# Four buffers for the attention's residual, with other banks, another steady order and another order of the first slots

## What is computed

```python
x = x + tanh(g_xattn[0]) * performer(layernorm(x), ctx, ctx)
x = x + tanh(g_ffn[0]) * ffn(layernorm(x))
# performer: 16 heads of 16, 64 random features, causal
proj_q, proj_k = (q * scale) @ random_features, (k * scale) @ random_features
h_k = -0.5 * sum(k * k);  k_stab = max(h_k)          # over all batches
q_prime = nc * (exp(proj_q) + 1e-4)
k_prime = nc * (exp(h_k + proj_k - k_stab) + 1e-4)
out = causal(q_prime @ k_prime.T) @ v / causal(q_prime @ k_prime.T).sum()
# ffn: attention of each token over its own 16 heads, then a soft mixture of 8 experts
x = x + (softmax(q @ k.T / 4) @ v) @ Wo + bo
gate = softmax(rmsnorm(x) @ Wg + bg)
return x + sum_e gate[e] * (rmsnorm(x) @ We[e])
```

## Time and profile before

| | us |
|---|---|
| median of 3 runs | 1058.45 (1058.41 to 1059.62) |
| the profiled execution | 1063.04 |
| its span | 1061.3 |
| TensorE busy in the span | 984.1 (93%) |
| VectorE, ScalarE, GpSimd busy | 885.9 (83%), 763.1 (72%), 793.3 (75%) |
| scores of batch 0, 4 and 7 begin | 45.74, 142.18, 239.16 |
| scores of batch 31 begin | 973.56 |

### The profile page before, as it was taken

How to read it: one execution, slowest core, us unless ns; L and a number is a source line. 1 busy time by engine, 2 the same in 40 slices (tenths; PEclk the granted TensorE clock), 3 DMA queues, 4 the chain that set the end, 5 groups by cost and what they waited for, 6 DMA issues and landing times.

```text
span 1061.3 us, 35315 instructions
## 1 busy us (share of the span) xinstructions
PE 984.1 (93%) x14918; PEld 824.8 (78%) x14918; DVE 885.9 (83%) x1860; ACT 763.1 (72%) x1628; POOL 793.3 (75%) x1275
## 2 busy tenths in 40 slices
PE   0467899999999999999999999999999999999998
PEld 0346678888878888888888888888888888888787
DVE  6777888888988888889888888888888889887887
ACT  5669876678777777877767777776777877776541
POOL 4478887777878778778787877778778777887551
PEclk9989999999999999999999999999999999999999
DMA  9600001100111100101110000011100101100000
GB/s 294 188 22 22 29 15 32 32 12 22 32 32 32 32 21 23 32 22 32 32 32 32 13 31 24 30 32 32 32 29 15 32 22 32 32 22 12 12 12 31
DMA packets 39439, 38.89 MB, mean 37 GB/s; under 512 B 3953, under 2 KB 39025, under 8 KB 39281
## 3 DMA queue, kind: packets, MB, share of 16 engines
q1 hardware_dynamic: 38896, 36.59, 11.0%
q0 software_dynamic: 384, 0.04, 0.1%
HBM read 28.23 MB, written 8.39 MB: 35 GB/s over the span
## 4 chain that ended last, share of the span: by engine, by line
PE 65%; POOL 14%; DVE 9%; ACT 4%; DMA 4%; issue 3%; SPq 1%; POOLq 0%; ACTq 0%
PE ps L2454 12%; PE ps L2456 11%; PE ps L2455 11%; PE ps L2499 7%; PE ps L2487 6%; PE ps L2469 4%; PE ps L2448 4%; PE ps L2533 3%; DMA c_in<-in_ctx 3%; PE ps L2509 2%; PE ps L2524 2%; DVE z L1528 2%; PE ps L2492 2%; DVE hk L1866 1%; POOL x L466 1%
## 5 line engine op out<-in xcount | busy, mean ns | idle before, releaser
L1528 DVE SCALAR_TENSOR_TENSOR z<-ps,gate,z 128x256 f32<-128x256 f32 x512 | 239.6, 473 | 28.6 <-POOL gate L550 16.2
L2454 PE MATMUL ps<-we_hi,h_hi 128*128 128x512 f32 (+2 forms) x640 | 237.9, 372 | 0.3 <-DVE qkv L1645 0.3
L2456 PE MATMUL ps<-we_hi,h_lo 128*128 128x512 f32 (+2 forms) x640 | 224.4, 351 | 0.0
L2455 PE MATMUL ps<-we_lo,h_hi 128*128 128x512 f32 (+2 forms) x640 | 224.1, 350 | 0.0
L2487 PE MATMUL ps<-qf,kf 64*64 64x192 f32 (+1 forms) x2048 | 152.2, 365 | 16.9 <-POOL kf L581 4.0
L2454 PEld LDWEIGHTS ps<-we_hi,h_hi 128*128 128x128 f32 x640 | 120.4, 188 | 26.5 <-issue 10.5
L2456 PEld LDWEIGHTS ps<-we_hi,h_lo 128*128 128x128 f32 x640 | 120.3, 188 | 17.3
L2455 PEld LDWEIGHTS ps<-we_lo,h_hi 128*128 128x128 f32 x640 | 120.8, 189 | 11.7
L2492 PEld LDWEIGHTS ps<-qf,kf 64*64 64x64 f32 x2048 | 106.3, 136 | 6.4
L2499 PE MATMUL ps<-att,v 128*32 128x256 f32 (+1 forms) x2048 | 103.4, 332 | 2.1 <-POOL att L521 1.2
L2492 PE MATMUL ps<-qf,kf 64*64 64x128 f32 (+1 forms) x2048 | 100.9, 247 | 0.0
(11 more groups left out here) (231 smaller groups left out, 3042.6 us busy)
## 6 DMA issues: line engine op xcount, KB each, us to landing
x_in<-in_x SPq DMA_DIRECT2D x32, 256.0 KB, 2.8
c_in<-in_ctx SPq DMA_DIRECT2D x64, 128.0 KB, 3.0
out<-z SPq DMA_DIRECT2D x32, 256.0 KB, 2.2
c_chunk<-in_ctx SPq DMA_DIRECT2D x14, 512.0 KB, 5.6
stage<-in_L_ffn_We SPq DMA_DIRECT2D x2, 1024.0 KB, 11.6
c_chunk<-in_ctx SPq DMA_DIRECT2D x2, 256.0 KB, 3.8
stage_o<-in_L_ffn_Wo SPq DMA_DIRECT2D x1, 256.0 KB, 3.5
stage_q<-in_L_ffn_Wq SPq DMA_DIRECT2D x1, 256.0 KB, 12.7
```

The costliest lines, as they stand in the source:

```text
L1528: return dve.scalar_tensor_tensor(out=z[b % 2][:, t, :], in0=ps[:, bank, offset:offset + D], scalar=gate[:, t, ex:ex + 1], in1=z[b % 2][:, ...
L2454: pe.matmul(out, a_hi(c), b_hi(c), start=(c == 0), stop=False)
L2455: pe.matmul(out, a_hi(c), b_lo(c), start=False, stop=False)
L2456: last = pe.matmul(out, a_lo(c), b_hi(c), start=False, stop=(c == C - 1))
```

## The change

It has four parts; kinds, sizes and number of the computing instructions stay the same.

- `x1` has four buffers where it had two. Its step no longer waits for `z0` of two batches before, and waits for `o_x` in every batch. In POOL's slot it moves from behind `z0` to behind `o_n`.
- `BANK` gives other banks to `av0`, `fk0`, `fk3`, `fq0`, `fq1`, `fq2`, `fq3`, `kv1`, `mm01`, `mm0g`, `mm1g`, `o`, `qq`, `s`, `x010`, `x011`, `x110`, `x111`, `y01`, `y10`, `y11`. The semaphores are grouped anew and the conditional waits follow the new orders.
- The slot of each engine has another order. SP's issues the context first and the store last. POOL's puts `k_lo` and `m11`, besides `g_r`, `m10` and `r2`, ahead of `v_bd`, and gate, v1, pk2, m00, m01, q_r at its end, which is where the next period begins. DVE's has `q_bn` ahead of `g_bn`, and `c_t` behind `a01`. ACT's has `k_bd` ahead of `x000`. PE's changes a few neighbours (`mm1g` for `mm0g` first, `kv1` ahead of `kv0`, `mm12` ahead of `mm11`).
- The first slots are written in another order, with more of them written out on PE, POOL and ACT; their last parts are now part of the loop's order. On PE, `mm03` stands right behind `mm02` for batch 31, and behind only `h2_t.31` for batch 30, where `mm11` and `mm12`, or others, stood between them.

```diff
-BANK = dict(av0=0, av1=3, dn=5, first=0, fk0=0, fk1=6, fk2=4, fk3=5, fq0=4, fq1=2, fq2=7, fq3=3, h2=0, ht=1, kv0=7,
-            kv1=6, mm00=4, mm01=0, mm02=7, mm03=7, mm0g=0, mm10=5, mm11=6, mm12=3, mm13=6, mm1g=1, nd0=2, nd1=3, o=4,
-            otr=4, pv0=1, pv1=2, qq=1, s=5, stab=0, x000=1, x001=7, x010=5, x011=4, x100=4, x101=2, x110=7, x111=3,
-            y00=0, y01=2, y10=1, y11=6)
+BANK = dict(av0=5, av1=3, dn=5, first=0, fk0=5, fk1=6, fk2=4, fk3=0, fq0=2, fq1=3, fq2=4, fq3=7, h2=0, ht=1, kv0=7,
+            kv1=3, mm00=4, mm01=2, mm02=7, mm03=7, mm0g=1, mm10=5, mm11=6, mm12=3, mm13=6, mm1g=0, nd0=2, nd1=3, o=2,
+            otr=4, pv0=1, pv1=2, qq=6, s=0, stab=0, x000=1, x001=7, x010=2, x011=5, x100=4, x101=2, x110=6, x111=1,
+            y00=0, y01=4, y10=7, y11=3)
...
-        x1 = [sb(f"x1_{p}", [P, T, D]) for p in range(2)]
+        x1 = [sb(f"x1_{p}", [P, T, D]) for p in range(4)]
...
-                store_(n - 4)
-                load_x_(n + 2)
                 load_c_(n + 3)
+                load_x_(n + 2)
+                store_(n - 4)
...
-                if b in (0, 1, 4):
-                    pool.wait_ge(*at("o_x", b))
-                if b >= 2:
-                    pool.wait_ge(*at("z0", b - 2))
-                pool.tensor_tensor(x1[b % 2][:, :, :], o_x[:, :, :], x_in[b % 2][:, :, :], ALU.add).then_inc(*up("x1", b))
+                pool.wait_ge(*at("o_x", b))
+                pool.tensor_tensor(x1[b % 4][:, :, :], o_x[:, :, :], x_in[b % 2][:, :, :], ALU.add).then_inc(*up("x1", b))
...
-                if b in (3, 4, 29, 30, 31):
-                    pool.wait_ge(*at("v_t", b))
+                pool.wait_ge(*at("v_t", b))
```

2459 lines of the change are left out of this document (1433 added, 1026 removed).

## The result

| | median, us | runs |
|---|---|---|
| before | 1060.77 (1058.09 to 1064.85) | 22 |
| after | 1065.59 (1061.74 to 1068.41) | 22 |

The ratio is 1.0042 [1.0031, 1.0052]: 0.4% slower, where 1055.0 and "faster" were forecast. The forecast started from 1058.45, the median of 3 runs of the kernel before; over these 22 it is 1060.77, and 2.3 of the 10.6 us between 1055.0 and 1065.59 are that difference. The profiled execution of the changed kernel took 1066.27 us, 1064.3 of them in the span, 0.7 above its median; the one of before was 2.3 above the median of these 22 runs.

A forecast was written before the change was run, and what follows sets the result against it. Bound: mostly TensorE's own work in the steady part, with waits at the start, in four batches and the tail. Terms −3.3 − 3.0 + 1.4 + 1.5 = −3.4 took 1058.45 to 1055.0 us; range 1047 to 1061.5.

The forecast's parts named there:

- Start, −3.3: Up to batch 0's scores: VectorE fills and a statistic moved into idle time save 4.2, POOL's added steps cost 0.9.
- Slots 0 to 3, −3.0: Batches 0 to 3: 2.3 us from ACT's scalings and q_lo.1 moved, 0.7 more by batch 4; bounds −5 to +1.
- that is 2.3 us on the scores of batch 1: Batch 0: two ACT weight scalings leave the exponentials' way, q_lo.1 fills POOL's idle time; batch 1's scores gain 2.3 us.
- Steady part, +1.4: 24 regular periods: −5.8 from c_in waits gone, +7.2 from pv waiting for POOL's v_bd; bounds −5.8 to +5.
- 24 × 0.3: Steady part: POOL's longer chain to v_bd starts pv 0.3 us late in each of 24 periods, +7.2.
- what is then late is nothing on this engine: Steady part, VectorE: context load issued first ends 14 c_in waits; TensorE returns to 30.36 us periods, up to −5.8.
- x1 and banks, 0: Steady part: four x1 buffers worth nothing themselves; other banks cost 0, bounded at 0 to 0.1 us a period.
- Tail, +1.5: After the steady part: TensorE waits of 3.9 to 5 us (mm03, mm1g, pv) against 3.0 before; bounds 0 to +3.
- A: Rival, steady part: POOL's chain keeps up and v_bd never holds pv; −10.6, 1047.9 us; chance 0.20.
- C: Rival, steady part: v_bd costs over 0.5 us each period; at 0.6, +3.8, 1062.3 us, slower; chance 0.16.
- B: Rival: gains of start and slots 0 to 3 given back before steady part; +0.9, 1059.4; 0.26 with forecast's upper edge.
- D: Rival: steady part unchanged at 30.60 us a period; 1053.7 us, inside the forecast; chance 0.38 together with the forecast.

The follow-up runs named there:

- b_fill: Kernel before with the new kernel's start on VectorE (fills and first statistic ahead of c_t.0, sel_h ahead of first sum) and load_x.0 first: 1057.95 us, ratio 0.9968.
- a_fill: Kernel after with its VectorE start put back (fills, first statistic and sel_h behind the first context and first sum): 1073.09 us, ratio 1.009 to the kernel before.
- a_wehi: Kernel after with ACT's scalings we_hi3 and we_hi1 put back between batch 0's score tiles, gamma2 ahead of the stabilizer: 1067.19 us, ratio 1.0037 to the kernel before.
- b_x1: Kernel before with x1 in four buffers instead of two, its step not waiting for z0 of two batches before: 1061.52 us, ratio 0.9988.

## Why the prediction was wrong

**Start, −3.3: right.** −3.4 in the profile. As an edit of its own (b_fill) it gave −3.9, and 0.32% of the whole; POOL's order is left alone there, so by the prediction's sum it would be the −4.2 of VectorE. The sum of fills taken out of VectorE's busy chain was a sound way to read the earlier trace rows. It does not tell what the old order costs in the new kernel (7.1, a_fill).

**Slots 0 to 3, −3.0: wrong.** +0.3. The step that failed is "that is 2.3 us on the scores of batch 1", added to a layout with old durations. The scores of batch 1 did come earlier in the profile (17.98 us behind batch 0, where it was 20.12). But the scalings were not what had held them: put back (a_wehi), they moved the scores of batch 1 by 1.0 at most. And the gain did not last: batch 2 took 28.02 us where it had taken 24.50, and TensorE's idle time over the four batches stayed at 20 to 21 us. The prediction's bounds allowed for this, a wait of one engine for another "may take it all". Two executions of the kernel after differ by 2.6 us here (96.74 and 94.15) with the clock, so a term of 3 us in this stretch can't be read from one pair of profiles' lengths.

**Steady part, +1.4: wrong by 2.8.** It came at +4.2 in this pair, and at some +7 over the eight profiles named under the result. V_bd was sized right in the loop: 0.3 forecast, 0.34 measured by the move of k_lo. What failed was (a) "24 × 0.3" as the whole price of the new order. Only 17 of the 24 periods run in POOL's loop order; seven are written out in another, and four of them, 10 to 13, took 2.8 us more than before. In three of those pv waited for v_bd as well, 0.20 to 0.39, behind waits for x and for the stored z that the sum has no term for. The section on the change says that more slots were written out, but the prediction let the loop's order stand for them. And (b) "what is then late is nothing on this engine; TensorE comes back to the regular 30.36". The load of x was put behind a load that waits, and its first reader put ahead of g_bn; when x lands late, the period is 31.4 to 32.5. Nor were the c_in waits worth 5.8: alone, in the kernel before, taking them away gave back 1.0 to 3.2. The last 16 periods came out at +1.8 where the prediction's figure for 24, +1.4, would give +0.9.

**x1 and banks, 0: right** as far as tried; x1 was (b_x1).

**Tail, +1.5: right in kind and nearly in size,** +1.9. The waits named are there, on TensorE's timeline of the new kernel:

```profile
1009.83 1.16 PE L2804 MATMUL ps<-v_bd,p_t 128*32 128x68 f32 x64 [1.13 <-DVE ht_lo L2083]
...
1029.84 1.15 PE L2804 MATMUL ps<-v_bd,p_t 128*32 128x68 f32 x64 [0.86 <-DVE z L1803]
1032.99 0.39 PE L2725 MATMUL ps<-we_hi,h_hi 128*128 128x264 f32 x1 [0.71 <-DVE h_lo L1859]
...
1046.82 0.39 PE L2725 MATMUL ps<-we_hi,h_hi 128*128 128x256 f32 x1 [0.73 <-DVE z L1803]
...
1059.48 0.39 PE L2725 MATMUL ps<-we_hi,h_hi 128*128 128x256 f32 x1 [1.17 <-DVE z L1803]
```

The last two are mm03 of 30 and of 31, put at 0.6 and 1.1; the 0.71 is mm1g.30. The five add up to 4.6, within the 3.9 to 5 of the forecast, but in part by luck: the mis-sized terms are pv, 0.4 each in the forecast and 1.13 and 0.86 here, and the 0.7 for mm1g.31, which didn't come. With h2_t put ahead of pv and mm13.29 ahead of mm1g.30 the tail is 1.3 shorter.

**Rivals.** A fell with pv's 0.34. C had the right sign by another road: it asked for more than 0.5 a period at v_bd, and v_bd stayed at 0.34; the written-out periods and the late x made up the rest. B's mechanism was right as to batches 0 to 3 and no more. D kept the steady mean at 30.60; it came at 738.61 / 24 = 30.78.

**What stays open.** The medians differ by 4.8 us and the two profiled executions by 3.2. The other profiles of the two steady orders say that this pair is a mild one (+7.2 over batches 7 to 30, not +4.2), which is more than the 1.6 us between them; how often x and z land late in an execution without a profile is not known. The regular period without the v_bd wait is 30.27 and not the old 30.36; 0.09 has no cause shown. What makes period 12 of the written-out part 31.04, without a wait at v_bd, is not shown. The banks were not tried alone, and neither was the third buffer for x with the seam mended.

## What to carry to other kernels

Count for how many periods an order really holds: a kernel with a written-out part and a loop has a seam, and one seam that doesn't fit cost 4.8 us here, where five more periods in the loop's order won 2.1. Where a step is moved ahead of another on a busy helper engine, add up that engine's chain to the next step which the bound engine waits for; it held to 0.04 us here, and moving one step of 1.3 us off that chain, with a seam that fits, a third buffer for the input and a mended tail, turned 0.4% slower into 0.8 to 1.1% faster. Before a loss of 3 us is read from one pair of profiles, see what a second profile of the same kernel shows: here the stretch of batches 0 to 3 moved by 2.6 us, and the steady part by 3.7, without a change. When a wait for one transfer is removed by reordering one queue, look at each of the other transfers on it (x, then the store, here), since one of them takes the last place.
